# A graph network on one core: one fixed item per tile, edges counted by comparing keys, own rows on VectorE

## The chip, the core and the metric

The kernel runs on one core of a Trainium2 chip. Its engines work side by side and meet through semaphores: TensorE (PE; its weight loads are PEld), VectorE (DVE), ScalarE (ACT), GpSimd (POOL) and SyncE (SP), which here issues the plain transfers. POOL issues the gathers, transfers whose row addresses come from a table. The metric is the device time of one execution in microseconds (us), lower is better.

## The reference

50000 nodes with 256 features, 25000 directed edges, four graph layers one after another, each followed by a residual and a layer norm:

```python
x = layernorm(x + L0(x))            # sum of weight*x[dst] by src, linear, norm, relu
x = layernorm(x + L1(x, 16 kinds))  # two relational layers:
#   for each kind r: s = segment_sum(x[src]*(kind==r), dst)
#                    cnt = segment_sum(kind==r, dst)
#                    out += blockdiag(W[r]) applied to s / max(cnt, 1)
x = layernorm(x + L2(x, 24 kinds))  # two attention hops:
#   e = leaky(sum(([x[src], x[dst]] @ fc_w.T + fc_b) * rel[kind]))
#   w = softmax of e over the edges with the same src
#   x = segment_sum(x[dst]*w, src) + x;  x = x / norm(x)
x = layernorm(x + L3(x))            # interaction layer
```

## The kernel before

Nodes are cut into 391 tiles of 128 (TILES). `sort_edges` sorts the edges twice, by source and by destination, and writes records into *items*: an item holds up to 128 edges whose node is in one tile, one edge per partition. A tile has as many consecutive items as its edges need, at least one. Of these data (some 64 edges per tile) every tile has one item, so item t is tile t, but the program doesn't rely on it: `tables.make` computes for each item which tile to load (LOAD), where to store (STORE; the spare rows for all but a tile's last item), its tile's last item (LAST), whether it goes on from the item before (`keep`), and `number` computes the slot of its tile among the eight loaded (SLOT, `octet_row`). All engines read rows and slots from this table at run time, through registers.

The stages: constants and sort; `mean_layer` (l0); `count_edges_and_message` (ma); `relation_layer` (l1a); `message_phase` (mb); `relation_layer` (l1b); `attention_hop` twice (l2a, l2b); `interaction_layer` (l3). Each stage is one block in which every engine runs its own list of steps, written out in the program; there is no scheduler.

ma does two things. It makes the messages of the edges, chunk by chunk (216 chunks of 128 edges, sorted by kind, taken as 108 pairs): POOL gathers the source rows (L1098), TensorE transposes them (L1220), ScalarE copies (L1186), TensorE multiplies by the kind's block matrix (L1229), VectorE copies (L1120), SyncE stores; POOL can be 24 chunks ahead. And it finds for each edge how many edges have its destination and kind, since the mean divides by it. For 49 groups of 8 items, beside the first 48 pairs, VectorE makes one-hot matrices of node (L1111) and kind (L1106), TensorE multiplies them into counts (L1244) and ScalarE copies these (L1191). Then 16 scans over 640 items carry the counts from item to item (L1160), beside eight pairs, and in the next 48 pairs counts are looked up: the names of an item's nodes come in as rows (`ma_row`, 256 KB a group), VectorE compares them with the partition's number (`hot_t`, L1125), TensorE multiplies with the totals (L1253), and VectorE picks the kind's column (L1130, L1133). TensorE's fill in other stages is a product of zeros (`keep_busy`, L772); ma has none.

`attention_hop` works in octets of eight items. POOL gathers the eight neighbours' rows (L1989). VectorE builds the one-hot matrices and the scores (up to L2077). TensorE spreads scores and a mask over a 128x128 square per item (`spread`, L2298 and L2300), VectorE takes the maximum (L2126), and then carries a running maximum from item to item (scan L2130, `old_top`, `below` L2135, `empty`, `minus`). ScalarE takes the exponent (L2212) with its sum (`share`), and `shrink` from `minus` (L2204). TensorE turns the chances (L2307), looks up head scores (L2320) and aggregates the neighbours (L2288). The item's own row, weighted by its guarded sum, has to be added: in l2a VectorE does it (`add_self`, L2100) and then adds the item before (`add_up`, L2121: z = z_before*shrink + z). In l2b POOL makes eight diagonal matrices (L2022, L2025), TensorE multiplies them with x into the same sums (L2275), and VectorE's `add_up` (L2118) adds the item before. ScalarE squares and sums, and an inverse root follows (`inv_v` L2147, `inv_log` L1721), in l2b a second one for the layer norm (L2164). TensorE has 24 fill products an octet in l2b, 34 in l2a. The first 48 octets (24 hops) are written out one by one; what is beyond is a loop, which here runs once.

## Time and profile before

| what | us |
|---|---|
| median of 3 runs (6646.8 to 6664.31) | 6657.72 |
| span of the profiled execution, for which nothing else is given | 6924.1 |
| constants and sort | 0 to 544 |
| l0 | 552 to 1466 |
| ma | 1468 to 1896 |
| l1a | 1896 to 2594 |
| mb | 2595 to 2935 |
| l1b | 2935 to 3827 |
| l2a | 3828 to 4768 |
| l2b | 4768 to 5868 |
| l3 | 5868 to 6924 |

| engine | busy us | share |
|---|---|---|
| TensorE | 6036.3 | 87% |
| VectorE | 5018.1 | 72% |
| ScalarE | 4517.3 | 65% |
| POOL | 3702.0 | 53% |

The span is from the first to the last instruction of one profiled execution, a slower one than the timed runs. Busy time is summed over instructions. PEclk is the clock granted to TensorE as a share of full speed. An idle time before an instruction is put down to what ended it.

### The profile page before, as it was taken

Reading aid. Unit: us, or ns where it says so; the run is one execution under the profiler, and the core shown is the slowest. Engines: PE = TensorE matmul, PEld = TensorE weight load, DVE = VectorE, ACT = ScalarE, POOL = GpSimd, SP = SyncE. Lnnn points to the kernel's source line nnn. Section 1 sums busy time; section 2 is a strip of 40 time slices with the busy share of each in tenths; the row PEclk is TensorE's granted clock in tenths of the full one; section 3 lists DMA queues with packets and bytes.
Section 4 is the critical chain, followed back from the end, with each engine's and each line's share of the span. In section 5 each row is a group of like instructions: output and inputs, shape, how many; then the busy total and the mean of one; then the engine's idle time right before and its main releaser. Section 6 shows DMA issues by size and latency. Waiting matters only on the chain. (4 is left out here: it accounts for less than half of the span.)

```text
span 6924.1 us, 154954 instructions
## 1 busy us (share of the span) xinstructions
PE 6036.3 (87%) x34664; PEld 5008.9 (72%) x34665; DVE 5018.1 (72%) x17037; ACT 4517.3 (65%) x15396; POOL 3702.0 (53%) x3473
## 2 busy tenths in 40 slices
PE   6437999977899987899999788887888887999999
PEld 2226999966877775699999666665776766888888
DVE  9786999976555551277777677775666666898898
ACT  1866999952144441178888566665777776777777
POOL 0766777756366666544444444444554455444444
PEclk9658999988899998999999899998989998999999
DMA  1025777765566665577777566665666665444444
GB/s 39 2 6 162 211 210 211 211 187 163 164 184 189 192 182 166 163 215 220 218 221 219 167 203 201 198 200 158 206 198 194 196 203 175 117 127 125 126 126 119
DMA packets 1158773, 1173.00 MB, mean 169 GB/s; under 512 B 301535, under 2 KB 1032838, under 8 KB 1157701
## 3 DMA queue, kind: packets, MB, share of 16 engines
q1 hardware_dynamic: 1007108, 953.00, 45.3%
q0 software_dynamic: 151360, 216.47, 12.4%
q8 instruction: 127, 2.08, 0.1%
q14 instruction: 178, 1.45, 0.1%
HBM read 961.43 MB, written 392.14 MB: 195 GB/s over the span
## 5 line engine op out<-in xcount | busy, mean ns | idle before, releaser
L214 POOL DMA_INDIRECT landing_first<-messages,by_dst_meta x768 | 842.7, 1097 | 721.8 <-PE l1b_ps_b L1541 366.5
L214 POOL DMA_INDIRECT landing_last<-x,by_dst_meta x384 | 434.4, 1131 | 561.0 <-PE l_ps_a L1678 487.9
L1989 POOL DMA_INDIRECT landing_last<-z,by_src_meta x408 | 424.3, 1040 | 521.3 <-PE l2b_ps_g L2288 366.6
L1989 POOL DMA_INDIRECT landing_last<-x,by_src_meta x408 | 422.7, 1036 | 462.4 <-PE l2a_ps_g L2288 255.9
L214 POOL DMA_INDIRECT landing_first<-in_x,by_src_meta x384 | 407.7, 1062 | 196.7 <-PE l_ps_a L993 74.4
L1495 ACT ACTIVATE l1a_x_t<-l1a_ps_x,by_dst_first 128x256 f32<-128x256 f32 x400 | 168.0, 471 | 418.0 <-PE l1a_ps_x L1527 280.0
L1539 PE MATMUL l1b_ps_b<-root,l1b_x_t 128*128 128x256 f32 x1600 | 426.9, 389 | 1.4
L1539 PE MATMUL l1a_ps_b<-root,l1a_x_t 128*128 128x256 f32 x1584 | 418.1, 386 | 9.7 <-issue 6.1
L1003 PE MATMUL l_ps_b<-l_w,l_both 128*128 128x256 f32 x1624 | 419.3, 381 | 0.0
L1006 PE MATMUL l_ps_b<-l_w,l_agg_t 128*128 128x256 f32 x1624 | 418.0, 380 | 0.0
L1697 PE MATMUL l_ps_b<-l_w,l_mix_t 128*128 128x256 f32 x1592 | 396.6, 392 | 10.2 <-issue 7.7
L1447 DVE SCALAR_TENSOR_TENSOR l1a_total<-l1a_total,by_dst_keep,l1a_ps_b 128x256 f32<-128x256 f32 x394 | 187.1, 475 | 292.1 <-PE l1a_ps_b L1541 234.5
L1693 PE MATMUL l_ps_b<-l_w,l_x_t 128*128 128x256 f32 x1592 | 382.2, 383 | 2.5 <-ACT l_x_t L1658 2.5
L1697 PEld LDWEIGHTS l_ps_b<-l_w,l_mix_t 128*128 128x128 f32 x1592 | 286.2, 189 | 115.7 <-DVE l_mix_t L1614 63.1
L288 POOL DMA_INDIRECT item_records<-sort_rec,places x196 | 218.5, 1115 | 243.8 <-DVE places L596 184.5
L1006 PEld LDWEIGHTS l_ps_b<-l_w,l_agg_t 128*128 128x128 f32 x1624 | 309.6, 191 | 42.5
L1098 POOL DMA_INDIRECT landing_first<-x,rel_index x216 | 238.7, 1105 | 164.4 <-PE ma_ps_x L1220 83.9
L1539 PEld LDWEIGHTS l1a_ps_b<-root,l1a_x_t 128*128 128x128 f32 x1584 | 286.3, 191 | 55.0 <-issue 18.9
L772 PE MATMUL l2a_ps_g<-zero_row,ones_b 128*128 128x392 bf16 x1734 | 321.2, 329 | 1.1 <-issue 1.1
L1003 PEld LDWEIGHTS l_ps_b<-l_w,l_both 128*128 128x128 f32 x1624 | 294.1, 191 | 32.1
L1539 PEld LDWEIGHTS l1b_ps_b<-root,l1b_x_t 128*128 128x128 f32 x1600 | 289.6, 191 | 36.5 <-issue 3.7
L1693 PEld LDWEIGHTS l_ps_b<-l_w,l_x_t 128*128 128x128 f32 x1592 | 286.6, 190 | 33.8 <-ACT l_x_t L1658 2.9
(399 smaller groups left out, 19392.5 us busy)
## 6 DMA issues: line engine op xcount, KB each, us to landing
l_both<-in_x_both SPq DMA_DIRECT2D x416, 256.0 KB
l2a_x<-x SPq DMA_DIRECT2D x53, 1216.0 KB
z<-l2a_result SPq DMA_DIRECT2D x400, 152.0 KB
x<-l1b_result SPq DMA_DIRECT2D x392, 152.0 KB
l2b_x<-z SPq DMA_DIRECT2D x53, 1024.0 KB
l1b_x<-h SPq DMA_DIRECT2D x408, 128.0 KB
l1b_res<-x SPq DMA_DIRECT2D x408, 128.0 KB
l2b_res<-x SPq DMA_DIRECT2D x51, 1024.0 KB
```

Of the source, the lines that this page charges most:

```text
L214: pool.indirect_dma_start(gathered[:, slot, 0:D], None, source[0:count, :], bass.IndirectOffsetOnAxis(ap=rows, axis=0), bounds_check=limit ...
L288: self.pool.indirect_dma_start(self.target, bass.IndirectOffsetOnAxis(ap=self.place[:, column:column + 1], axis=0), self.source(column), N ...
L772: pe.matmul(spare, c.ones_b[:], c.zero_row[:], start=True, stop=True)
L1003: pe.matmul(ps_b[k % 4], x_t[:, m, i * P:(i + 1) * P], w[:, 2 + i, :], start=(i == 0), stop=False)
L1006: last = pe.matmul(ps_b[k % 4], agg_t[:, k, i * P:(i + 1) * P], w[:, i, :], start=False, stop=(i == 1))
L1098: pool.indirect_dma_start(gathered[:, slot, :], None, x_in[0:N_NODES, :], bass.IndirectOffsetOnAxis(ap=relations.index[:, chunk:chunk + 1] ...
L1447: dve.scalar_tensor_tensor(total[:, k, :], total[:, (k - 1) % RING, :], graph.keep[:, bass.ds(j, 1)], ps_b[k // 2 % 2][:, k % 2, :], ALU.m ...
L1495: act.activation(x_t[:, k, :], ps_x[k // 2 % 2][:, k % 2, :], ACT.Copy, scale=graph.first[:, bass.ds(j, 1)]).then_inc(s["xt"], 1)
L1539: pe.matmul(sums, x_t[:, k, f * P:(f + 1) * P], root[:, f, :], start=(f == 0), stop=False)
L1693: pe.matmul(ps_b[k % 4], x_t[:, k, i * P:(i + 1) * P], w1[:, i, :], start=(i == 0), stop=False)
L1697: last = pe.matmul(ps_b[k % 4], mix_t[:, k, i * P:(i + 1) * P], w2[:, i, :], start=False, stop=(i == 1))
L1989: pool.indirect_dma_start(gathered[:, k, :], None, x_in[0:N_NODES, :], bass.IndirectOffsetOnAxis(ap=rows, axis=0), bounds_check=limit, oob ...
```

## The change

Items are now laid out at fixed places: item t (t < 391) is the first item of tile t, MAIN = 392, and only tiles with more than 128 edges get all their items from number 392 on (there are none here). The item arrays grow from 640 to 896. SLOT, `octet_row` and `number` are gone. The 48 written-out octets read loads, heads and residual at constant addresses and do no scan, no `shrink`, no `add_up`; a guard is made from the maximum (`guard`). Only the loop's octets keep the carried sums, and they load each tile by its own transfer. In l2b the own rows move from POOL and TensorE to VectorE (`add_self`). In ma the 384 fixed items are counted in another way: a key is node*16 + kind; the keys of an item are loaded as a row on all partitions, and one VectorE operation per item compares the row with the partition's own key and sums the hits. The old counting with products stays for the groups from item 384 on (one here), ahead of the pairs. The look-ups shrink to one loop round of two groups. In `mean_layer` two buffers move into unused memory; its work stays.

```diff
+MAIN = TILES + 1
+MAX_ITEMS = MAIN + 2 * (N_EDGES // (P + 1))
...
+OCTETS_FIXED = HOPS_FIXED * 2
...
@@ sort_edges, buckets of each of two orders
-                    chain.step(dve.tensor_scalar(b["count"][:], b["int2"][:], 1.0, None, ALU.max))
-                    chain.step(dve.tensor_tensor_scan(b["end"][:], c.ones_row[:], b["count"][:], 0.0, ALU.mult, ALU.add))
+                    chain.step(dve.tensor_copy(b["seed"][:], b["int2"][:]))
+                    chain.step(dve.scalar_tensor_tensor(b["count"][:], b["seed"][:], 2.0, b["seed"][:], ALU.is_ge, ALU.mult))
+                    chain.step(dve.tensor_tensor_scan(b["end"][:], c.ones_row[:], b["count"][:], float(MAIN), ALU.mult, ALU.add))
                     chain.step(dve.tensor_tensor(b["base"][:], b["end"][:], b["count"][:], ALU.subtract))
-                    dve.tensor_scalar(b["seed"][:], b["base"][:], float(P), None, ALU.mult).then_inc(s_start, 1)
+                    chain.step(dve.tensor_tensor(b["seed"][:], b["base"][:], c.iota[:], ALU.subtract))
+                    chain.step(dve.scalar_tensor_tensor(b["seed"][:], b["count"][:], 2.0, b["seed"][:], ALU.is_ge, ALU.mult))
+                    chain.step(dve.tensor_tensor(b["seed"][:], b["seed"][:], c.iota[:], ALU.add))
+                    dve.tensor_scalar(b["seed"][:], b["seed"][:], float(P), None, ALU.mult).then_inc(s_start, 1)
...
@@ first message stage, VectorE
+                def compare(g, odd):
+                    if not odd:
+                        dve.wait_ge(key_in[g % 2], (g // 2 + 1) * 16)
+                    for k in range(odd * HALF, (odd + 1) * HALF):
+                        j = g * RING + k
+                        if j >= 2:
+                            dve.wait_ge(s["compared"], j - 1)
+                        dve.tensor_scalar(same[:, j % 2, :], key_row[:, g % 2, k, :], key[:, j:j + 1], 0.0, ALU.is_equal, ALU.add,
+                                          accum_out=graph.share[:, j:j + 1]).then_inc(s["compared"], 1)
...
-                for pair in range(COUNTED):
-                    last = dve.tensor_tensor_scan(total[:, r, :], graph.keep[:], total[:, r, :], 0.0, ALU.mult, ALU.add)
+                    last = dve.tensor_tensor_scan(total[:, r, :], graph.keep[:, FAST:FAST + COUNTED], total[:, r, :], 0.0, ALU.mult, ALU.add)
                     if r % 2:
-                        take_message(COUNTED + r // 2)
+                        take_message(r // 2)
                 last.then_inc(s["summed"], 1)
-                look(0, 0, 0)
-                dve.wait_ge(s["kind2"], 1)
-                for pair in range(SCANNED, LOOKED):
-                    take_message(pair)
-                    g = pair - SCANNED
-                    look_and_take(g, g % 2, g // 2)
-                for pair in range(LOOKED, PAIRS_ALL):
-                    take_message(pair)
-                with dve.Fori(COUNTED // 2, (groups + 1) // 2) as both:
+                look(FAST, 0, FAST_GROUPS // 2)
+                dve.wait_ge(s["kind2"], FAST_GROUPS + 1)
+                with dve.Fori(FAST_GROUPS // 2, (groups + 1) // 2) as both:
                     for h in range(2):
                         look_and_take(both * 2 + h, h, both)
+                for pair in range(SCANS_AT, PAIRS_ALL):
+                    take_message(pair)
+                    g, odd = divmod(pair - FIRST_LOOK, 2)
+                    if 0 <= g < FAST_GROUPS:
+                        compare(g, odd)
...
@@ first message stage, TensorE
-                    if pair < COUNTED:
-                        count(pair)
-                    elif SCANNED <= pair < LOOKED:
-                        look_up(pair - SCANNED, (pair - SCANNED) % 2)
                     if pair + 2 < PAIRS_ALL:
                         turn(pair + 2)
-                    if pair == COUNTED - 1:
-                        with pe.Fori(COUNTED, groups) as g:
-                            count(g)
-                    if pair == SCANNED - 1:
+                    if pair == SCANS_AT - 1:
                         pe.wait_ge(s["summed"], 1)
-                with pe.Fori(COUNTED // 2, (groups + 1) // 2) as both:
-                    for h in range(2):
-                        look_up(both * 2 + h, h)
+                        with pe.Fori(FAST_GROUPS // 2, (groups + 1) // 2) as both:
+                            for h in range(2):
+                                look_up(both * 2 + h, h)
...
@@ attention_hop, loads on SyncE
+                def load_tiles(octet, target, source, columns, loads):
+                    if octet.general:
+                        rows = rows_of("load", LOAD, octet)
+                        for q in range(OCT):
+                            sp.dma_start(target[:, q, :], source[bass.ds(rows[q], P), columns]).then_inc(loads[1][octet.half], 16)
+                    else:
+                        tiles = source[bass.ds(octet.item * P, OCT * P), :].rearrange("(k p) d -> p k d", p=P)
+                        sp.dma_start(target, tiles[:, :, columns]).then_inc(loads[0][octet.half], 16)
...
@@ attention_hop, POOL
-                def diagonals(octet):
...
-                    pool.tensor_tensor(diag[:, 0:own_pe, :], c.ident[:].unsqueeze(1).broadcast_to([P, own_pe, P]),
-                                       guarded[:, octet.half, 0:own_pe].unsqueeze(2).broadcast_to([P, own_pe, P]), ALU.mult)\
-                        .then_inc(s["diag"], 1)
...
@@ attention_hop, VectorE
                 def guard(o):
                     pass_wait(dve, s, s["chance"], o.item + OCT)
-                    o.wait(dve, s["empty"])
-                    dve.tensor_tensor(guarded[:, o.half, :], share[:, o.both], empty[:, o.half, :], ALU.add).then_inc(s["guarded"], 1)
+                    if o.general:
+                        o.wait(dve, s["empty"])
+                        dve.tensor_tensor(guarded[:, o.half, :], share[:, o.both], empty[:, o.half, :], ALU.add)\
+                            .then_inc(s["guarded"], 1)
+                    else:
+                        dve.scalar_tensor_tensor(guarded[:, o.half, :], peak[:, o.both], FLOOR, share[:, o.both], ALU.is_le, ALU.add)\
+                            .then_inc(s["guarded"], 1)
...
-                        dve.scalar_tensor_tensor(like_sums(q, z[:, k, :]),
-                                                 like_sums(q, x[:, bass.ds(at[q] + o.base, 1), :].rearrange("p k d -> p (k d)")),
+                        dve.scalar_tensor_tensor(like_sums(q, z[:, k, :]), like_sums(q, x[:, k, :]),
                                                 guarded[:, o.half, q:q + 1], sums(q), ALU.mult, ALU.add).then_inc(s["mixed"], 1)
...
                 def add_up(o, h):
+                    if not o.general:
+                        return
...
                 def maximum(o):
                     o.wait(dve, s["e_done"])
-                    dve.tensor_reduce(peak[:], ps_e[:], AX.X, ALU.max).then_inc(s["peak"], 1)
+                    dve.tensor_reduce(peak[:, o.both], ps_e[:], AX.X, ALU.max).then_inc(s["peak"], 1)
+                    if not o.general:
+                        o.wait(dve, s["peak"])
+                        dve.tensor_scalar(below[:, o.half, :], peak[:, o.both], -1.0, -FLOOR, ALU.mult, ALU.min)\
+                            .then_inc(s["below"], 1)
+                        return
...
-                    steps = [(add_residual, 0), (find_slots, 1), (centre, 0), (scores, 2), (part(add_up, 0), 1), (have_variance, 0), (maximum, 2)]
-                    steps += [(part(add_self, 1), 1)] if own_dve else []
-                    steps += [(part(add_up, 1), 1), (find_nodes, 3), (have_square, 1), (lambda o: inv2.square(dve, o), 0),
-                             (lambda o: inv2.weigh(dve, o), 0), (lambda o: inv2.improve(dve, o), 0), (square, 1),
-                             (weigh, 1), (shift_bias, 0), (improve, 1)]
+                    steps = [(add_residual, 0), (centre, 0), (scores, 2), (guard, 1), (part(add_self, 0), 1), (part(add_up, 0), 1),
+                             (have_variance, 0), (maximum, 2), (part(add_self, 1), 1), (part(add_up, 1), 1), (find_nodes, 3),
+                             (have_square, 1), (lambda o: inv2.square(dve, o), 0), (lambda o: inv2.weigh(dve, o), 0),
+                             (lambda o: inv2.improve(dve, o), 0), (square, 1), (weigh, 1), (shift_bias, 0), (improve, 1)]
...
@@ attention_hop, TensorE, last hop
-                    steps = [(find_slots, 3), (find_own, 1), (part(own_rows, 0), 1), (part(aggregate, 0), 1), (part(own_rows, 1), 1)]
-                    steps += [(part(own_rows, 2), 1), (part(aggregate, 1), 1), (part(aggregate, 2), 1), (part(own_rows, 3), 1)] if not own_dve else [
-                              (part(aggregate, 1), 1), (part(aggregate, 2), 1)]
-                    steps += [(spread, 2), (part(aggregate, 3), 1), (part(fill, 16), 2), (part(turn_chances, 0), 2), (look_up, 3),
-                             (part(fill, 4), 2), (part(turn_chances, 1), 2), (part(fill, 4), 2)]
+                    steps = [(part(aggregate, 0), 1), (part(aggregate, 1), 1), (part(aggregate, 2), 1), (spread, 2), (part(aggregate, 3), 1),
+                             (part(fill, 16), 2), (part(turn_chances, 0), 2), (look_up, 3), (part(fill, 4), 2),
+                             (part(turn_chances, 1), 2), (part(fill, 4), 2)]
```

VectorE in l2b before, from an octet's scores to a later octet's one-hot matrices.

```order
L2077 SCALAR_TENSOR_TENSOR l2b_score<-l2b_plain 128x8
L2118 SCALAR_TENSOR_TENSOR l2b_z<-l2b_z,l2b_shrink,l2b_ps_g 128x256 x4
L2164 TENSOR_SCALAR l2b_inv_v<-l2b_norm_squares 128x8
L2126 TENSOR_REDUCE l2b_peak<-l2b_ps_e 128x8
L2130 SCALAR_TENSOR_TENSOR l2b_top<-l2b_restart,l2b_top,l2b_peak 128x8
L2133 TENSOR_TENSOR l2b_old_top<-l2b_top,l2b_restart 128x8
L2135 TENSOR_SCALAR l2b_below<-l2b_top 128x8
L2137 TENSOR_SCALAR l2b_empty<-l2b_top 128x8
L2140 TENSOR_TENSOR l2b_minus<-l2b_old_top,l2b_top 128x8
L2143 COPY l2b_top<-l2b_top 128x1
L2118 SCALAR_TENSOR_TENSOR l2b_z<-l2b_z,l2b_shrink,l2b_ps_g 128x256 x4
L2057 TENSOR_SCALAR l2b_hot_t<-l2b_row,item_id 128x1024
```

The same stretch of VectorE after.

```order
L2084 TENSOR_REDUCE l2b_plain<-l2b_own 128x8
L2086 SCALAR_TENSOR_TENSOR l2b_score<-l2b_plain 128x8
L2096 SCALAR_TENSOR_TENSOR l2b_guarded<-l2b_peak,l2b_share 128x8
L2109 SCALAR_TENSOR_TENSOR l2b_z<-l2b_x,l2b_guarded,l2b_ps_g 128x256 x4
L2169 TENSOR_SCALAR l2b_inv_v<-l2b_norm_squares 128x8
L2127 TENSOR_REDUCE l2b_peak<-l2b_ps_e 128x8
L2130 TENSOR_SCALAR l2b_below<-l2b_peak 128x8
L2109 SCALAR_TENSOR_TENSOR l2b_z<-l2b_x,l2b_guarded,l2b_ps_g 128x256 x4
L2066 TENSOR_SCALAR l2b_hot_t<-l2b_row,item_id 128x1024
L2068 TENSOR_SCALAR l2b_mask<-l2b_row,item_id 128x1024
```

The eight additions stand at the same places, now with x and `l2b_guarded` in the place of the item before; the scan and four short operations behind the maximum are gone, so `below` follows it, and `l2b_guarded` stands ahead of the additions, which POOL made before.

TensorE in l2b before: the start of an octet's aggregation (ISA rows set an address from a register).

```order
L1831 TENSOR_LOAD by_src_table x2
L1834 ISA
L2275 ISA
L2275 MATMUL l2b_ps_g<-l2b_x,l2b_diag 128x256
L2275 ISA
L2275 MATMUL l2b_ps_g<-l2b_x,l2b_diag 128x256
L2288 MATMUL l2b_ps_g<-landing_last,l2b_hot 128x256 x2
L1834 ISA
L2275 ISA
L2275 MATMUL l2b_ps_g<-l2b_x,l2b_diag 128x256
```

TensorE in l2b after, from the aggregation to the next octet's turned chances.

```order
L2272 MATMUL l2b_ps_g<-landing_last,l2b_hot 128x256 x6
L2282 MATMUL l2b_ps_e<-l2b_mask,ident_b 128x512
L2284 MATMUL l2b_ps_e<-ident,l2b_score 128x128 x4
L2282 MATMUL l2b_ps_e<-l2b_mask,ident_b 128x512
L2284 MATMUL l2b_ps_e<-ident,l2b_score 128x128 x4
L2272 MATMUL l2b_ps_g<-landing_last,l2b_hot 128x256 x2
L788 MATMUL l2b_ps_spare<-zero_row,ones_b 128x392 x16
L2291 MATMUL l2b_ps_e<-ident,l2b_chance 128x128 x4
```

The products with `l2b_diag` and the register rows between the aggregations are gone; six aggregations stand in one piece.

VectorE in ma before, in the pairs with look-ups.

```order
L1120 COPY ma_message<-ma_ps_m 128x512
L1125 TENSOR_SCALAR ma_hot_t<-ma_row,item_id 128x1024
L1106 TENSOR_TENSOR ma_kind<-by_dst_meta,iota 128x128
L1130 TENSOR_TENSOR ma_own<-ma_kind,ma_ps_e 128x128
L1133 TENSOR_REDUCE by_dst_share<-ma_own 128x8
L1120 COPY ma_message<-ma_ps_m 128x512
```

VectorE in ma after: the end of the loop round with look-ups, and the pairs with compares behind it, which go on in this way.

```order
L1176 TENSOR_REDUCE by_dst_share<-ma_own 128x8
L1181 REGISTER_ALU
L1210 ISA
L1210 COMPARE_AND_BRANCH
L1152 COPY ma_message<-ma_ps_m 128x512 x2
L1162 TENSOR_SCALAR ma_same,by_dst_share<-ma_key_row,ma_key 128x128 x4
L1152 COPY ma_message<-ma_ps_m 128x512
```

Between two message copies stood the wide comparison with the partition's number and the pick of a column, which waits for TensorE; now four compares stand there, which wait for no other engine.

## Rows read from the trace of the kernel before

**Rows 1.** Windows, one for each stage; the columns stand in the first row:

```profile
core 0: us, PE busy (x) PEld busy (x) DVE busy (x) ACT busy (x) POOL busy (x), PEclk, DMA share, GB/s
...
1466.00:1896.00 430.00, 324.19 (x2498) 300.57 (x2498) 255.88 (x531) 83.11 (x216) 238.68 (x216) 0.81 0.57 168
...
2934.00:3827.00 893.00, 879.46 (x5564) 800.78 (x5564) 647.10 (x2588) 719.76 (x1987) 428.42 (x408) 0.99 0.73 217
...
4768.00:5868.00 1100.00, 956.76 (x5186) 757.40 (x5186) 734.91 (x2420) 815.43 (x3207) 552.55 (x532) 0.90 0.64 194
```

**Rows 2.** What POOL waited for, 147 to 545 us: total, times, longest:

```profile
POOL item_records L288 <- DVE places L596: 184.5, 5, 152.8
```

**Rows 3.** Groups of VectorE's instructions by line and shape, 358 to 405 us:

```profile
L376 DVE TENSOR_SCALAR_CACHE_REDUCE sort_in_relation<-dst_end,item_id 128x391 f32<-128x391 f32 x5 | 3.1, 620 | 3.5 <-remote 2.2 <-DVE by_src_groups L396 1.3
...
L391 DVE TENSOR_TENSOR sort_tmp<-sort_tmp 128x5 f32<-128x5 f32 x2 | 0.3, 167 | 0.6 <-DVE sort_tmp L390 0.5
```

**Rows 4.** Windows inside the first message stage:

```profile
1500.00:1652.00 152.00, 99.62 (x917) 86.31 (x916) 101.33 (x234) 43.84 (x141) 112.30 (x100) 0.82 0.55 163
1685.00:1850.00 165.00, 154.57 (x1082) 151.32 (x1082) 80.49 (x191) 22.86 (x39) 79.53 (x76) 0.80 0.62 172
```

**Rows 5.** Line L1098, the gathers of the first message stage: ns, first and last start:

```profile
L1098 POOL DMA_INDIRECT landing_first<-x,rel_index x216: 1006/1012/1680, 1468.7 to 1847.5; - x108
```

**Rows 6.** Line L1329, the gathers of the second message stage:

```profile
L1329 POOL DMA_INDIRECT landing_first<-h,rel_index x216: 1004/1012/1027, 2595.0 to 2913.2; - x108
```

**Rows 7.** Groups by line and shape, 1466 to 1896 us, first message stage:

```profile
L1106 DVE TENSOR_TENSOR ma_kind<-by_dst_meta,iota 128x128 f32<-128x128 f32 x51 | 14.5, 284 | 0.0
```

**Rows 8.** Timeline of TensorE in the first message stage: start, length:

```profile
1673.74 1.15 PE L1229 MATMUL ma_ps_m<-ma_wide,ma_x_t 128*128 x8 [1.77 <-DVE ma_message L1120]
1674.73 0.60 PE L1220 MATMUL ma_ps_x<-ident,landing_first 128*128 128x128 f32 x4
1680.85 2.07 PE L1229 MATMUL ma_ps_m<-ma_wide,ma_x_t 128*128 x8 [5.51 <-DVE ma_message L1120]
...
1691.98 1.09 PE L1220 MATMUL ma_ps_x<-ident,landing_first 128*128 128x128 f32 x4
```

**Rows 9.** Windows inside the two attention stages:

```profile
3900.00:4600.00 700.00, 617.58 (x3927) 467.69 (x3927) 533.14 (x1381) 470.06 (x1804) 330.16 (x320) 0.99 0.66 200
4860.00:5760.00 900.00, 797.62 (x4311) 631.07 (x4309) 624.89 (x2065) 692.35 (x2717) 450.79 (x431) 0.91 0.66 199
```

**Rows 10.** Timeline of one octet of the first attention stage:

```profile
4329.97 0.67 PE L2288 MATMUL l2a_ps_s<-landing_last,l2a_hot 128*128 128x304 f32 x2
...
4331.47 1.01 POOL L1989 DMA_INDIRECT landing_last<-x,by_src_meta  x1 [4.83 <-PE l2a_ps_s L2288]
...
4339.26 4.87 SPq L1939 DMA_DIRECT2D z<-l2a_result  x8
...
4341.15 0.36 DVE L2070 TENSOR_TENSOR l2a_both<-l2a_ps_s,landing_last 128x192 f32<-128x192 f32 x1 [0.36 <-DMA landing_last<-x,by_src_meta]
...
4346.31 0.68 PE L2288 MATMUL l2a_ps_s<-landing_last,l2a_hot 128*128 128x304 f32 x2
```

**Rows 11.** Waits in the first attention stage, 3900 to 4600 us:

```profile
ACT l2a_chance L2212 <- DVE l2a_below L2135: 62.8, 40, 2.7
...
DVE l2a_both L2070 <- DMA landing_last<-x,by_src_meta: 23.8, 31, 2.4
```

**Rows 12.** Groups by line and shape, 4860 to 5760 us, second attention stage:

```profile
L2275 PE MATMUL l2b_ps_g<-l2b_x,l2b_diag 128*128 x692 | 186.1, 404 | 19.2 <-POOL l2b_diag L2025 17.4 <-issue 1.6
...
L2212 ACT ACTIVATE l2b_chance<-l2b_ps_e,l2b_below 128x128 f32<-128x128 f32 x344 | 121.0, 377 | 83.0 <-DVE l2b_below L2135 41.6 <-issue 41.4
...
L2025 POOL TENSOR_TENSOR l2b_diag<-ident,l2b_guarded 128x1024 f32<-128x1024 f32 x44 | 83.9, 1906 | 3.4
...
L2147 DVE TENSOR_SCALAR l2b_inv_v<-l2b_total_sq 128x8 f32<-128x8 f32 x44 | 45.6, 1038 | 83.6 <-DMA x<-l1b_result 38.2 <-ACT l2b_squares L2199 34.1 <-issue 11.3
...
L1721 ACT ACTIVATE l2b_inv_log<-l2b_inv_v 128x8 f32<-128x8 f32 x87 | 17.6, 202 | 72.1 <-DVE l2b_inv_v L2147 68.5 <-issue 3.0
```

420 lines of the change are left out of this document (191 added, 229 removed).

## Prediction

> **What bounds the kernel now.** I read the page's busy shares first: TensorE is busy 87% of the span, VectorE 72%, ScalarE 65%, POOL 53%, so no engine is full all the time and the bound has to be found stage by stage. I then cut the span into stages with the windows view (the stage table above, its rows for three stages in [rows 1]), and inside each stage read the groups by line and shape, the waits and one octet or pair on the timeline. The change touches the sort, the first message stage (430 us), the first attention stage (941 us) and the second (1100 us). The other stages issue the same work as before and I leave them at their time.
>
> In the sort POOL waits 184.5 us for VectorE's places, 152.8 of it in one piece [rows 2]: VectorE is on the path before the scatters.
>
> In the first message stage the time changes hands twice. While counts are made (1500 to 1652 us) 100 gathers take 152 us, 1.52 each. While the counts are looked up (1685 to 1850) TensorE is busy 154.6 of 165 us and only 76 gathers are issued, 2.17 each [rows 4]. The look-up is what fills TensorE there, at a mean granted clock of 0.80. The second message stage does the same messages with no counting: its 216 gathers start from 2595.0 to 2913.2, 1.48 each [rows 6], against 1468.7 to 1847.5, 1.76 each, in the first [rows 5].
>
> In the first attention stage 320 gathers are 40 octets in 700 us, 17.5 us each, with TensorE busy 15.4, VectorE 13.3, ScalarE 11.8 [rows 9]. No engine is full; what closes is a loop. An octet's aggregation ends at 4330.64 (4329.97 + 0.67), that frees slots and a gather starts at 4331.47, VectorE sees the landing at 4341.15, then come scores, spread and the next aggregation, which ends at 4346.99 [rows 10]: 16.35 us.
>
> In the second attention stage 344 chances are 43 octets in 900 us, 20.9 us each, with TensorE busy 18.5, ScalarE 16.1, VectorE 14.5 [rows 9, 12]. ScalarE is idle 83.0 us before the chances, half of it put on VectorE's `below`, and 72.1 before `inv_log`, which waits for VectorE's `inv_v` [rows 12]. That op is 8 elements wide and yet takes 1038 ns, while POOL runs the diagonals, 1906 ns each, once per octet. VectorE's short op stands behind POOL's long one.
>
> **The change part by part.** The sums go against the profiled execution, whose span is 6924.1 us; the page gives no time outside the span. The median of the runs is 6657.72, 3.8% less, so I scale the sum by 6657.72/6924.1 = 0.962.
>
> Sort: four more bucket operations per direction, eight in all. The nearest row is a 391-wide operation of 0.620 us [rows 3]: +5.0. The tables need 36 wide reductions instead of 30, +3.7, and about 28 more operations of the 0.167 kind, +4.7 [rows 3]. With the gaps of a dependent chain I take +15, from +8 (the scatters cover part, since those in flight while the tables are made don't wait) to +30 (every small operation pays a wait). The item records grow from 640 to 896 rows and are loaded before the first layer: 0.7 MB at the 168 GB/s of [rows 1] is 4 us, part of it covered by the weights' loads; I take +2.5, between 0 and +5.
>
> First message stage: the 16 look-up products per pair on TensorE go, and so do nearly all counts and their copies. What is left on TensorE per pair is four transposes and eight products, 0.60 + 1.15 = 1.75 us at full clock and 1.09 + 2.07 = 3.16 at the half one [rows 8]. VectorE gets 384 compares of 128 columns with an accumulator. The trace has none of this form. A 128x128 operation without accumulator takes 0.284 [rows 7], a 391-wide one with it 0.620 [rows 3]. I take 0.35, four per pair, 1.4 us, plus a message copy near 0.7: 2.1 per pair on VectorE, below POOL's pair. The bound above, 0.620, gives 3.2 per pair, which would be VectorE-bound: 96 pairs x 3.2 = 307 us. So POOL sets the pace as in the second message stage: first start 1468.7, 215 x 1.48 = 318, and a tail of 22 (the second message stage ends at 2935, its last gather starts at 2913.2) end at 1809, against 1896: -87. The second message stage has no key loads, though: each two pairs load 256 KB broadcast over the partitions, the bytes of the row loads before. With them the count stretch ran 1.52 and moved 163 GB/s, so they may cost something. I add 15 for that and for the compares beside POOL. Result -72, bounds -87 and -30. The upper bound is VectorE or TensorE at 3.2 per pair for the 96 pairs with compares, 307, with some 40 us of first pairs and scans, and the tail of 48 that the stage had (1847.5 to 1896): 395 us of 430, in round numbers.
>
> The trace doesn't show how compares and gathers share memory. In the count stretch, where VectorE is busy 101.3 of 152 us, POOL's gathers are 1.12 each instead of 1.01 [rows 4, 6]. The Trainium skill, page "SBUF — State Buffer", section "Who interferes with whom", says that the `tensor_scalar` form that writes out its accumulator does not take the port pair shared with GpSimd, unlike the plain form. By the rule the compares would not lengthen a gather, and the 15 us above would shrink towards 0; by the row of the count stretch they would cost 0.11 x 216 = 24. No run here shows it yet.
>
> First attention stage: VectorE loses eight operations over 304 columns and five small ones per octet. VectorE is not the bound. ScalarE's waits for `below` are 62.8 us over 40 octets, 1.6 each [rows 11], and those mostly go, but the gather loop of 16.35 stays whole: none of its links is removed. It also carries landings that come late (23.8 us over 31 waits, 0.6 per octet [rows 11]). I take 16.8 us instead of 17.4: 49 octets x 0.6 = -29; bounds -34 (everything at 16.7) and 0 (the landing sets it as now).
>
> Second attention stage, the largest term. Per octet:
> TensorE loses the own-row products, 186.1/43 = 4.3 us [rows 12], and the register work ahead of them: 18.5 becomes 14.2. POOL loses the diagonals (1.9). VectorE issues as many 256-wide additions as before, with x in the place of the carried sum, and loses scan, `old_top`, `empty` and `minus`. ScalarE loses one 8-wide activation (0.2, as L1721's shape): 16.1 becomes 15.9, and is now the fullest engine. Of ScalarE's 4.8 us idle (900 - 692.35 over 43), `inv_log` has 72.1/43 = 1.7, of which I let 1.5 go because `inv_v` no longer stands behind the diagonals (0.83 for the operation alone, the rest its queue), and chances have 83.0/43 = 1.9, of which 1.3 goes since `below` follows the reduction directly. 15.9 + 4.8 - 2.8 = 17.9, and I take 18.1 for the longer way of `guard`, which now stands on VectorE between scores and additions. (20.9 - 18.1) x 49 = -137; bounds T = 16.5 (-216, ScalarE full but for 0.6) and T = 20.0 (-44, if transfers hold it).
>
> Cover lost: own rows were products that kept TensorE awake, see the rival below. The last, general octets load x, heads and residual with eight DMAs instead of one; SyncE needs 4.87/8 = 0.61 per issue [rows 10], 21 more per octet in the last hop, on a queue that runs ahead by octets: +6, between 0 and +15. Stores wait behind them.
>
> Sum: 15 + 2.5 - 72 - 29 - 137 + 6 = -214.5; scaled -206: 6658 - 206 = 6452 us.
>
> **The rivals.**
> B, transfers take over. The second attention stage moves 199 GB/s now [rows 9]; at 18.1 us an octet it would need 230. The most in any stage is 217 GB/s, in the second relation stage [rows 1]. At 217 the octet is 20.9 x 199/217 = 19.2, and since its loads stand in bursts I take 19.5: -69. With the message stage at -40 and the first attention stage at -10 the sum is -95, scaled -91: 6567 us. For it: late landings are already seen [rows 11]. Against: DMA share is 0.66, not 0.73 as in that stage.
> C, all at the floors: -216, -87, -34, and +20 for sort and loads: -317, scaled -305: 6353 us. Against: the remaining waits of a chain through five engines rarely vanish together.
> D, slower: the clock of TensorE falls in the second attention stage. It is granted 0.91 there now, with 89% busy [rows 9], and without the own rows TensorE works 14.2 us of 18.1. At 1.2 GHz throughout the 14.2 us become 14.2 x 0.91 x 2 = 25.8 us, more than any other engine has, and the octet lasts 25.8: +240 there, with the rest -77, so +163, scaled +157: 6815 us. It decides once the mean granted clock is under 14.2 x 0.91/20.9 = 0.62. For it: after 5.51 us without work the clock halved in the message stage (eight products 1.15 before, 2.07 after [rows 8]). Against: 24 fill products remain in each octet, and the gaps get shorter, not longer. The Trainium skill, page "TensorE: Matmul & The Clock Gate", section "HAM oscillation — how this bites in real kernels", states that an engine whose bursts are shorter than the waits between them is gated down again each time. By this rule the loss of the own rows speaks for D; the trace of the half-speed products agrees with the mechanism, not with its taking hold in an octet that is 78% busy.
> E, the fixed path gains nothing because the path it shortens isn't the one that ends last (the sort's +15 and message stage's compares at 0.620 eat the rest): -20 to +20, 6658.
>
> **How the numbers follow.** Forecast 0.60, B 0.21, C 0.10, D 0.04, E 0.05. The forecast's own range is 6400 to 6520; B reaches to 6600, C to 6350, so 6350 to 6600 holds about 0.85. A change of 0.3% (20 us) is about what can be told from none. Faster: 0.60 + 0.21 + 0.10 + a little of E = 0.92; same 0.03; slower 0.05.
>
> **What would show it.** The first message stage should last about 358 us with gathers at 1.48 to 1.55 us and POOL no longer waiting for the transposes for long; a compare between 0.28 and 0.62 us. The second attention stage should come at about 960 us, ScalarE the fullest, `inv_v` near 0.2 us, and no POOL work beside the gathers. The first attention stage should be 910 us with VectorE near 8.5 us of each octet. If the second attention stage stays above 1050 us, with ScalarE and TensorE idle before a landing, B was right; if TensorE's clock there is under 0.7, D. If the sort grows by more than 30 us, my chain costs are wrong.

## The result and the profile after

The changed kernel runs in 6409.3 us (median of 4 runs, 6406.93 to 6410.99); the kernel before ran in 6653.1 us beside it. The ratio is 0.963, 95% interval 0.9617 to 0.9644: 3.7% faster, 244 us. The forecast was 6452 us, 206 us less. The time lies in the range.

```profile
span 6409.2 us, 146244 instructions
...
PE 5644.9 (88%) x32700; PEld 4709.4 (73%) x32701; DVE 4652.7 (73%) x16722; ACT 4457.7 (70%) x15208; POOL 3534.5 (55%) x3365
...
PEclk9668999998899999999999899998999998999999
```

The page of the kernel after: span, busy time, and the rows by slices. TensorE is as full as before (88% of the span, 87% then). In the five slices that lie whole in the second attention stage the core moves 234 to 252 GB/s, where it moved some 200 before.

One thing has to be known before stages are compared. The kernel before was timed on several chips: on one of them seven runs took 6904 to 6935 us ("the slower chip" below), on two others 6632 to 6650 ("the faster chips"). The profile that the prediction rests on has a span of 6924.1 us and stages as long as those of the slower chip; this result is from a chip on which the kernel before took 6653.1. A second profile of the kernel before, on a faster chip, has a span of 6637.0 us. The table has the time from each stage's first gather or load to the next one's. The changed kernel itself was not run on the slower chip: there the column after is put together from kernels of the experiments in which that stage is the changed kernel's, unaltered. By that column the change gains as much on the slower chip (some 3.5%), but not in the same stages. The stages of the two faster profiles differ by 227.8 us in all, the medians of the runs by 244; the 16 us between them stand in no stage.

| stage | before, 6637.0 us | after, 6409.2 us | difference | slower chip: before, 6924.1 us | slower chip: after | difference |
|---|---|---|---|---|---|---|
| sort | 518.8 | 519.6 | +0.8 | 556.1 | 563.0 to 574.5 | +7 to +18 |
| l0 | 903.3 | 903.3 | 0.0 | 912.6 | 915 | +2 |
| ma | 397.6 | 300.4 | -97.2 | 428.7 | 348.5 to 350.4 | -79 |
| l1a | 675.7 | 681.8 | +6.1 | 697.6 | 698 | 0 |
| mb | 292.4 | 290.6 | -1.8 | 341.1 | 342 | +1 |
| l1b | 883.6 | 883.9 | +0.3 | 893.6 | 891 to 896 | -3 to +3 |
| l2a | 918.3 | 873.3 | -45.0 | 942.4 | 937 | -5 |
| l2b | 1002.9 | 907.0 | -95.9 | 1100.5 | 932.3 to 934.3 | -167 |
| l3 | 1044.4 | 1049.3 | +4.9 | 1051.5 | 1047 | -4 |

The stages l1a and l3 issue the same work in both; between the changed kernel and its variants on the faster chips they lie at 669.5 to 681.8 and 1044.8 to 1049.3 us, so 5 us there mean nothing.

The windows of the kernel after that answer to [rows 1, 4, 9], columns as there: the first message stage, the second one, and stretches inside the first and second attention stage.

```profile
1422.00:1722.00 300.00, 202.32 (x1350) 179.28 (x1350) 209.56 (x916) 67.45 (x124) 220.35 (x216) 0.85 0.81 242
2404.00:2697.00 293.00, 258.44 (x1872) 204.60 (x1872) 75.59 (x111) 63.37 (x108) 216.93 (x217) 0.97 0.64 192
3650.00:4350.00 700.00, 656.78 (x4260) 505.32 (x4259) 368.03 (x954) 493.67 (x1913) 349.89 (x350) 1.00 0.71 216
4530.00:5250.00 720.00, 606.61 (x3623) 487.06 (x3624) 526.57 (x1900) 683.94 (x2678) 361.22 (x347) 0.92 0.82 248
```

The same four places in the second profile of the kernel before:

```profile
1422.00:1819.00 397.00, 314.88 (x2498) 296.15 (x2498) 253.56 (x532) 83.99 (x216) 240.55 (x216) 0.84 0.61 182
2495.00:2787.00 292.00, 259.37 (x1872) 205.15 (x1872) 74.68 (x108) 63.20 (x108) 217.85 (x216) 0.97 0.64 192
3800.00:4500.00 700.00, 610.82 (x3978) 475.15 (x4017) 544.07 (x1416) 484.70 (x1846) 335.47 (x328) 1.00 0.67 205
4690.00:5410.00 720.00, 661.98 (x3774) 524.97 (x3811) 548.86 (x1811) 612.39 (x2397) 402.53 (x383) 0.96 0.72 220
```

The second attention stage: 344 chances in 720 us are 43 octets, 16.7 us each, against 38 (304 additions) in 720, 18.9 us each. VectorE is busy 12.2 us an octet after and 14.4 before. ScalarE is busy 95% of the stretch. TensorE's clock fell from 0.96 to 0.92. The first attention stage: 350 gathers, 43.7 octets, 16.0 us each, against 41 (328 gathers), 17.1 us each.

TensorE's only waits in these two stretches of the first attention stage, before and then after, are for the scores (total, times, longest):

```profile
PE l2a_ps_e L2300 <- DVE l2a_score L2077: 89.1, 41, 3.3
```

```profile
PE l2a_ps_e L2282 <- DVE l2a_score L2086: 43.2, 43, 2.2
```

That is 2.2 us an octet before and 1.0 after, while TensorE's work stays near 15 us an octet, fill products included: the octet of the first attention stage got shorter by what TensorE waits less for VectorE's scores.

Groups of the kernel after, first message stage, which answer to [rows 5, 7]: the gathers, and the compares, which are the new operation.

```profile
L1130 POOL DMA_INDIRECT landing_first<-x,rel_index x216 | 220.4, 1020 | 86.7 <-issue 55.4 <-POOLq L124 21.2 <-PE ma_ps_x L1255 10.1
...
L1162 DVE TENSOR_SCALAR_CACHE_REDUCE ma_same<-ma_key_row,ma_key 128x128 bf16<-128x128 f16 x384 | 109.4, 341 | 13.4 <-DMA ma_key_row<-node_rows 13.3
...
L1162 DVE DVE_READ_ACCUMULATOR ma_same<-ma_key_row,ma_key 128x1 f32 x384 | 31.8, 83 | 0.0
```

A compare takes 341 ns (0.35 was forecast) and 83 more to read the accumulator. Gathers wait 10.1 us for TensorE in all (55.1 in the second profile of before); 216 of them start in 284.9 us, 1.33 us each.

Groups of the second attention stage after, which answer to [rows 12]:

```profile
L2160 DVE SCALAR_TENSOR_TENSOR l2b_result<-l2b_z,l2b_inv_root,l2b_res 128x256 f32<-128x256 f32 x344 | 143.8, 482 | 15.4 <-DVE l2b_inv_root L1775 10.5 <-DMA l2b_res<-x 4.9
L2109 DVE SCALAR_TENSOR_TENSOR l2b_z<-l2b_x,l2b_guarded,l2b_ps_g 128x256 f32<-128x256 f32 x347 | 143.4, 475 | 11.8 <-DVE l2b_guarded L2096 11.8
...
L2221 ACT ACTIVATE l2b_chance<-l2b_ps_e,l2b_below 128x128 f32<-128x128 f32 x344 | 120.7, 375 | 15.2 <-DVE l2b_below L2130 15.0
...
L2282 PE MATMUL l2b_ps_e<-l2b_mask,ident_b 128*128 128x512 bf16 x88 | 42.4, 482 | 102.8 <-DVE l2b_score L2086 102.8
...
L1758 ACT ACTIVATE l2b_inv_log<-l2b_inv_v 128x8 f32<-128x8 f32 x86 | 17.4, 203 | 10.6 <-DVE l2b_inv_v L2153 10.6
...
L2282 PEld LDWEIGHTS l2b_ps_e<-l2b_mask,ident_b 128*128 128x128 bf16 x88 | 9.9, 112 | 120.4 <-DVE l2b_score L2086 120.4
...
L2153 DVE TENSOR_SCALAR l2b_inv_v<-l2b_total_sq 128x8 f32<-128x8 f32 x43 | 7.8, 182 | 77.5 <-ACT l2b_squares L2206 77.5
```

`inv_v` takes 182 ns, ScalarE waits 10.6 us for it and 15.0 for `below`. In [rows 12], over 900 us, these two were 68.5 and 41.6, but in the second profile of the kernel before, 4690 to 5410 us, they were only 4.0 and 52.6. What is new is TensorE's wait for the scores, 102.8 us.

### The profile page after: what moved, and what is told of

Read it like the earlier page. It is cut to its first block and busy times, and to the rows that moved or that the text cites. A ratio compares the mean times of both kernels' runs of the same rounds, so it can differ in the third digit from the quotient of the medians.

```text
span 6409.2 us, 146244 instructions
## 1 busy us (share of the span) xinstructions
PE 5644.9 (88%) x32700; PEld 4709.4 (73%) x32701; DVE 4652.7 (73%) x16722; ACT 4457.7 (70%) x15208; POOL 3534.5 (55%) x3365
## 5 line engine op out<-in xcount | busy, mean ns | idle before, releaser
L215 POOL DMA_INDIRECT landing_first<-messages,by_dst_meta x768 | 826.4, 1076 | 665.2 <-PE l1b_ps_b L1578 368.2
L843 ACT ACTIVATE l_norm_junk<-l_summed,l_norm_minus_mean 128x256 f32<-128x256 f32 x392 | 196.0, 500 | 139.2 <-DVE l_norm_minus_mean L834 139.2
```

What stands on the lines that cost most here:

```text
L215: pool.indirect_dma_start(gathered[:, slot, 0:D], None, source[0:count, :], bass.IndirectOffsetOnAxis(ap=rows, axis=0), bounds_check=limit ...
L843: act.activation(self.junk[:, k % self.junk_slots, :], values[:, k, :], ACT.Square, bias=self.minus_mean[:, k:k + 1], accum_out=self.squar ...
```

## Experiments

All but before_again are edits of the changed kernel, timed beside the kernel before; the ratio is to that. before_again, lookups_back, carry_back and own_rows_back ran on one of the faster chips, own_rows_2, pool_diag_2, pe_own_2 and apply4 on the other, and no_compare, pool_diag_only, pe_own_only and idle_adds on the slower chip. Differences of a stage are against the changed kernel's stage on a faster chip (873.3 and 907.0 us for the attention stages) or against the column of the slower chip. The six runs of own_rows, pool_diag and pe_own also keep ScalarE's array of squares in bf16 instead of f32, to make room; an operation on it takes 423 to 425 ns either way.

**before_again** is the kernel before without an edit.

> The kernel before, unchanged, for a second profile. Theory: the profiled execution of 6924 us was 4% slower than the runs because it was a slowed one, also where the two kernels issue the same work. Then a new profile lies near 6650 us, and the second message stage, whose code is the same in both kernels, gathers at about 1.31 us (281 us for 216) as in the kernel after, not at 1.48. Rival: the second message stage is really slower in the kernel before, by something that the ma stage leaves behind; then it stays at 1.48. What remains between this profile and the one after is the change: I expect the first message stage at 400 us against 300, the first attention stage at 900 against 870, the second at 1050 against 908.

One run of 6638.78 us, span 6637.0. The second message stage takes 292.4 us (gathers at 1.31 us) as in the kernel after, so its 341 is nothing that the code of the kernel before does. The theory held in its numbers. Its "slowed execution" turned out to be the slower chip, where kernels with this stage unchanged take 341.7 to 342.5 us for it. The first message stage came at 398, the first attention stage, forecast at 900, at 918, and the second, forecast at 1050, at 1003.

**lookups_back** puts eight look-up products of the old shape in 48 pairs of the first message stage.

```diff
+ if FIRST_LOOK <= pair < FIRST_LOOK + FAST_GROUPS:
+     for k in range(RING):
+         pe.matmul(ps_dummy[:, k * R1:(k + 1) * R1], hot_t[:, 1, k, :],
+                   total[:, :, k:k + 1]..., start=True, stop=True)
```

> The changed kernel with eight idle look-up products (sixteen passes of 128x16) put back on TensorE in 48 pairs of the first message stage, in the places where the look-ups stood; their results are used by nobody. Own theory (the look-ups made TensorE the bound): pairs of 3.6 to 4.3 us in place of 2.6, +50 to +85 us in that stage, clock in it lower or equal. Rival (the loads and VectorE's waits held the stage before, not TensorE): under +15 us.

6419.24 us, ratio 0.9665 (0.9649 to 0.9681); first message stage 325.3 us, +25. The window:

```profile
1500.00:1690.00 190.00, 180.14 (x1583) 174.41 (x1581) 122.82 (x638) 43.01 (x74) 129.69 (x130) 1.00 0.81 233
```

TensorE is full (180 of 190 us) at a clock of 1.00, and a pair takes 3.07 us on its timeline. So TensorE did become the bound, as the theory said, but for 25 us and not for 50 to 85, and with a higher clock and not a lower one (0.88 in the same stretch of the kernel after). TensorE of before_again, start and length in us, two pairs with look-ups and the products of a third:

```profile
1700.88 3.59 PE L1253 MATMUL ma_ps_e<-ma_total,ma_hot_t 128*128 x16
1704.31 1.09 PE L1220 MATMUL ma_ps_x<-ident,landing_first 128*128 128x128 f32 x4
1705.19 1.89 PE L1229 MATMUL ma_ps_m<-ma_wide,ma_x_t 128*128 x8
1706.90 1.88 PE L1253 MATMUL ma_ps_e<-ma_total,ma_hot_t 128*128 x16
1708.62 0.63 PE L1220 MATMUL ma_ps_x<-ident,landing_first 128*128 128x128 f32 x4
1709.09 1.06 PE L1229 MATMUL ma_ps_m<-ma_wide,ma_x_t 128*128 x8
```

The look-ups at 3.59, the transposes at 1.09 and the products at 1.89, 6.57 us together, are at 1.2 GHz; then the same at 1.88, 0.63 and 1.06, 3.57 together, at 2.4 GHz. The mean pair takes 4.2 us there (66 gathers in 140 us), at a granted clock of 0.81. VectorE waits for the names in that stretch, 1640 to 1780 us (total, times, longest):

```profile
DVE ma_hot_t L1125 <- DMA ma_row<-node_rows: 38.6, 25, 2.4
```

TensorE's products wait 7.0 us there for the comparison that follows the names, and its weight loads 10.7 us for nothing that the profile shows.

Products alone cost 25 of the 97 us. The other 72 are not taken apart by an experiment, so their cause is not shown. The profiles show two candidates. One is the half clock and the waits for name rows (together 1.1 us a pair over 3.07). The other is that in the count stretch gathers last longer, beside VectorE's `tensor_tensor` operations that make the one-hot matrices. The groups of POOL are at 1450 to 1600 us of before_again and, beside the compares, at 1500 to 1690 us of the kernel after:

```profile
L1098 POOL DMA_INDIRECT landing_first<-x,rel_index x101 | 119.7, 1185 | 30.8 <-issue 26.5 <-PE ma_ps_x L1220 4.3
```

```profile
L1130 POOL DMA_INDIRECT landing_first<-x,rel_index x146 | 146.1, 1000 | 44.5 <-issue 36.5 <-PE ma_ps_x L1255 7.9
```

**no_compare** leaves out the compares and their key loads (the counts stay at one, so messages are not divided).

```diff
- if 0 <= g < FAST_GROUPS:
-     compare(g, odd)
```

> The changed kernel without the 384 compares and without the key loads of the first message stage (12 MB less in transfers); the counts stay at one, so messages aren't divided by them. Theory (POOL's gathers set the pace at 1.3 us each, compares run beside them): first message stage within 6 us of 300. Rival (compares take the memory ports from POOL, or the key loads delay the landings of the gathers): 15 to 25 us shorter.

On the slower chip 6684.81 us against 6925.23 for before, ratio 0.9664 (0.9634 to 0.9695). Its first message stage lasts 344.6 us, against 348.5 to 350.4 in the three other kernels of this chip. Compares and key loads cost 4 to 6 us together; they run beside the gathers. The forecast 300 was for a faster chip; that the stage would move by no more than 6 us held. What the compares cost on a faster chip, where POOL is quicker, was not tried.

**carry_back** brings back the carried sums in the written-out octets of both hops.

```diff
 def add_up(o, h):
-    if not o.general:
-        return
 def maximum(o):
-    if not o.general: ... return        # below from the peak alone
 def measure(o, first, n):
-    act.wait_ge(s["mixed"], j + 1)
+    act.wait_ge(s["added"], j + 2)
```

> The changed kernel with the carried sums back in the 48 written-out octets of both hops: scan, old_top, empty, minus, shrink and add_up on VectorE, all else as after. Own theory (the first hop is held by its gather loop, the second by ScalarE): first hop +0.6 to +1.0 us per octet, +30 to +50 us; second hop: VectorE rises from 12.2 to about 17.4 us an octet, above ScalarE's 15.9, so the octet goes from 16.7 to about 19, +110 us. Sum +150 us, near 6560. Rival (transfers hold both hops, VectorE's work is free): under +30 us. Rival (everything VectorE loses was on the path): +5.2 us an octet in both, +500 us.

6683.22 us, ratio 1.0065 (1.0048 to 1.0082): slower than the kernel before. First attention stage 921.4, +48, which is all of the 45 us that it had gained. TensorE's wait for the scores is back there as well, 3650 to 4350 us:

```profile
PE l2a_ps_e L2268 <- DVE l2a_score L2086: 88.3, 41, 3.1
```

So in this stage the carried sums on VectorE stood between TensorE and its scores. Second attention stage 1140.1, +233, more than twice what was expected. There VectorE now adds twice for each item, the own row and then the item before, 16 additions an octet; the kernel before had one addition for both, since TensorE made the own rows. So this stage is not the one of the kernel before. Windows in the second and the first of them:

```profile
4600.00:5500.00 900.00, 717.43 (x3457) 566.86 (x3498) 682.39 (x2341) 669.65 (x2640) 341.38 (x336) 0.77 0.64 192
3650.00:4350.00 700.00, 611.67 (x3978) 478.36 (x4017) 540.47 (x1415) 480.61 (x1846) 336.51 (x329) 0.99 0.68 205
```

42 octets in 900 us are 21.4 us each, and no engine is full: VectorE 76%, ScalarE 74%. The granted clock of TensorE is 0.77, the lowest of all stretches here, though above the 0.7 that the prediction had named as the sign of its rival D. How much of the 233 us the clock costs, and how much the longer chain over VectorE, is not shown.

**own_rows_back** and **own_rows_2** are one kernel, run twice: the own rows of the second hop by POOL's diagonals and TensorE's products, with no carried sums; VectorE's additions stay, with a factor of zero. POOL also makes `guarded`, as before, and VectorE one 8-wide operation (`empty`) for it.

```diff
+ pool.tensor_tensor(diag[:], ident..., guarded[:, octet.half, :]..., ALU.mult)
+ pe.matmul(out, diag[:, q, :], x[:, k, cols], start=(q % 2 == 0), stop=False)
- dve...(z, x, guarded[:, o.half, q:q + 1], sums(q), ALU.mult, ALU.add)
+ dve...(z, x, nothing[:], sums(q), ALU.mult, ALU.add)
```

> The changed kernel with the own rows of the second hop made by POOL's diagonals and TensorE's products again, no carried sums. VectorE still issues its eight additions (with a factor of zero). Own theory (POOL's diagonals hold up VectorE's short operations and TensorE has 4.3 us more per octet): second hop from 16.7 to 19.5 us an octet, +137 us, inv_v back to about 1 us, near 6550. Rival (the carried sums and not the own rows were what cost): under +30 us. The other stages unchanged.

> The own rows of the second hop back on POOL and TensorE, as in own_rows_back, beside the two single parts on one chip. If each part cost by itself what it did alone (79 and 90 us), and they add up, the second hop is 165 us longer than after; if both lie in one chain and TensorE is the bound with either, 80 to 95.

6489.08 us, 0.9774 (0.9758 to 0.9791), and 6487.75, 0.9769 (0.9753 to 0.9785). The second attention stage is 990.4 and 990.3 us, +83: 87% of the stage's gain is the own rows' move. 13 us are left for all else in this stage, the scan and short operations of the carried sums and the constant addresses; the carried sums needed no additions of their own there. Expected were 137, and `inv_v` at about 1 us, which stayed at 172 ns.

**pool_diag_only** and **pool_diag_2**: POOL makes an idle array of the diagonals' shape once per octet; nobody waits.

```diff
+ pool.wait_ge(s["chance"], octet.item + OCT)
+ pool.tensor_tensor(diag[:], ident..., graph.keep[:, 0:OCT]..., ALU.mult)
```

> The changed kernel, and in the second hop POOL makes an idle array of the diagonals' shape (128x1024, ident times a column) once per octet at the place of the diagonals; nobody waits for it. Theory of the prediction (VectorE's short operations stand behind it, inv_v at 1 us): second hop +40 to +80 us. Rival, from the second profile of the kernel before, where inv_v took 196 ns beside the diagonals: under +12 us, and inv_v near 0.2 us.

> POOL's idle diagonals alone, again. Theory (what POOL's 1.9 us cost depends on whether they fall on VectorE's short operations and on the gathers' issue; the machine on which the first profile of before was taken is the one on which the short operations fell behind them): second hop +10 to +80 us, with inv_v's mean above 0.3 us where it is long and near 0.2 where it is short. Rival (the cost is POOL's own time in the gather loop, independent of VectorE): +70 to +80 us again, inv_v near 0.2 us.

On the slower chip 6764.63 us, 0.9779 (0.9757 to 0.9801), second attention stage 1012.4, +79, with `inv_v` at 1342 ns: the theory held there. On the faster 6506.57, 0.9794 (0.9777 to 0.981), 1007.1, +100, 2.0 us an octet for 1.9 us on POOL. Where these go, in VectorE's groups of pool_diag_2, 4530 to 5250 us:

```profile
L2168 DVE TENSOR_SCALAR l2b_inv_v<-l2b_total_sq 128x8 f32<-128x8 f32 x39 | 54.4, 1396 | 66.2 <-ACT l2b_squares L2221 66.2
...
L1770 DVE SCALAR_TENSOR_TENSOR l2b_inv_b<-l2b_inv_a,l2b_inv_v 128x8 f32<-128x8 f32 x78 | 43.2, 553 | 2.9
```

`inv_v` takes 1396 ns instead of 182, and `inv_b` 553 instead of 167. VectorE's busy time goes from 12.2 to 14.3 us an octet, though it does the same work. In own_rows_2 `inv_v` is short and the residual's additions are long (482 in the kernel after):

```profile
L2187 DVE SCALAR_TENSOR_TENSOR l2b_result<-l2b_z,l2b_inv_root,l2b_res 128x256 f32<-128x256 f32 x316 | 187.5, 654 | 10.8 <-DVE l2b_inv_root L1775 10.8
```

and so in before_again, where 305 of them at 137 ns more are 1.1 us an octet:

```profile
L2155 DVE SCALAR_TENSOR_TENSOR l2b_result<-l2b_z,l2b_inv_root,l2b_res 128x256 f32<-128x256 f32 x305 | 170.8, 619 | 17.2 <-DVE l2b_inv_root L1738 17.2
...
L2025 POOL TENSOR_TENSOR l2b_diag<-ident,l2b_guarded 128x1024 f32<-128x1024 f32 x39 | 74.4, 1907 | 3.1
...
L2147 DVE TENSOR_SCALAR l2b_inv_v<-l2b_total_sq 128x8 f32<-128x8 f32 x38 | 7.5, 196 | 44.4 <-ACT l2b_squares L2199 44.4
```

So in each of these profiles VectorE instructions are longer beside POOL's diagonal, by 1 to 2 us an octet together; which instruction pays differs, also between two profiles of the kernel before (`inv_v` 1038 ns in one, 196 in the other). The second expectation forecast 10 to 80 us by the chip, its rival 70 to 80 with a short `inv_v`; 100 us with a long one is neither.

**pe_own_only** and **pe_own_2**: TensorE multiplies with eight zero matrices at the places of the own-row products; POOL does nothing.

```diff
+ pe.matmul(out, diag[:, q, :], x[:, k, cols], start=(q % 2 == 0), stop=False)   # diag is zero
```

> The changed kernel, and in the second hop TensorE multiplies x with eight constant zero matrices into the sums, sixteen passes an octet, where the own-row products stood; POOL makes nothing, VectorE still adds the own rows. Theory (TensorE's 4.2 us are on the path: 14.1 + 4.2 = 18.3 us an octet against ScalarE's 15.9): second hop +75 to +90 us, nearly all of what bringing back both cost (83). Rival (TensorE has slack, only POOL's diagonals in its chain cost): under +25 us.

> TensorE's sixteen idle own-row passes alone, again. Theory (TensorE becomes the bound at 18.3 us an octet): second hop +75 to +90 us also here. Rival (it depends on the machine as POOL's part does): under +50 us.

On the slower chip 6779.89 us, 0.9798 (0.9778 to 0.9817), second attention stage 1023.5, +90: as expected. On the faster 6384.27 us, 0.9612 (0.9595 to 0.9628), stage 887.7: 19 us *less* than after. That missed the theory, and the rival had it. Its window:

```profile
4530.00:5250.00 720.00, 713.82 (x4414) 598.41 (x4457) 540.81 (x1959) 701.82 (x2774) 366.66 (x359) 1.00 0.84 255
```

The clock is 1.00 instead of 0.92, an octet takes 16.0 us, ScalarE is busy 97% and TensorE 99%. The idle products take 3.9 us an octet (174.5 us for 45), and all other products together went from 14.1 to 12.0. The spread products, which VectorE's maximum and the chances wait for, show it, first the kernel after and then pe_own_2:

```profile
L2284 PE MATMUL l2b_ps_e<-ident,l2b_score 128*128 128x128 f32 x697 | 126.0, 341 | 0.0
```

```profile
L2296 PE MATMUL l2b_ps_e<-ident,l2b_score 128*128 128x128 f32 x720 | 94.9, 275 | 5.7 <-DVE l2b_score L2087 3.4
```

They take 341 ns in the mean behind the wait for the scores, and 275 where the idle products fill that wait (TensorE's 102.8 us for the scores are 3.4 here). Work that yields nothing makes the stage shorter. 6384 is the lowest median of all kernels here, but it was not timed side by side with the changed kernel (6409), and the intervals of the two ratios overlap (0.9617 to 0.9628). Why the same edit costs 90 us on the slower chip stays open; at 4750 to 5470 us there TensorE is busy 93% at a clock of 0.95, and VectorE's `inv_v` waits 35.3 us for a landing of x, which it does not on the faster chip.

The three edits together on that faster chip: the idle diagonals cost 100 us, the idle products gain 19, and both with their real use (own_rows_2) cost 83, close to the 81 of the sum. So there the gain from moving the own rows is about what POOL's diagonals had cost. The 80 to 95 us that the expectation of own_rows_2 gives for TensorE as the bound held in the number, by luck, and not in the reason. On the slower chip, where each part alone costs 79 and 90, the two together were not run.

**idle_adds**: in the first hop VectorE does eight additions of `add_up`'s shape into an array that nobody reads.

```diff
+ dve.scalar_tensor_tensor(idle[:], z[:, (k - 1) % HOP, :], guarded[:, o.half, 0:1], z[:, k, :], ALU.mult, ALU.add)
```

> The changed kernel, and in the first hop VectorE does eight additions of the shape of add_up in its place, each after the one before, into an array that nobody reads; scan, below and shrink stay out. Bringing back all of the carried sums cost 48 us there. Theory (the additions stand ahead of the next scores on VectorE and so in the gather loop): +30 to +45 us. Rival (the longer way to below and ScalarE's wait for the added sums cost): under +12 us.

On the slower chip 6682.47 us, 0.9655 (0.9635 to 0.9675); first attention stage 940.4 against 936.7 to 937.6 of the other three, +3. But the whole change gives that stage only 5 us there. Its theory missed and its rival held. But the run can't say what part of the carried sums made up the 45 on the faster chip: there TensorE waited for the scores (89.1 us before), while in the first profile of before its 64.5 us at the same place are put down to nothing that the profile shows and only 12.7 to the scores.

**apply4** moves the last normalisation of four items an octet from ScalarE to VectorE, to beat both kernels.

```diff
+ dve.tensor_scalar(result[:, k, :], result[:, k, :], inv2.root[:, k:k + 1], norm.bias[:, k:k + 1],
+                   ALU.mult, ALU.add).then_inc(s["out_dve"], 1)        # at the end of VectorE's steps
```

> The changed kernel, and in the second hop VectorE does the last normalisation (scale and bias, L2241) of four of the eight items, ScalarE the other four. Theory (ScalarE, busy 95% of the second hop after, is its bound): ScalarE loses 2.0 us of 16.7 per octet, VectorE gains 1 to 2 of its 12.2; octet at 15.0 to 15.5 us, second hop 60 to 80 us shorter, ratio to the kernel before 0.951 to 0.954. Rival (transfers at 248 GB/s or the gather loop hold it as much as ScalarE): under 20 us.

6446.62 us, 0.9708 (0.9691 to 0.9724), faster than the kernel before and slower than the changed one; second attention stage 956.8, +50. Window and wait:

```profile
4530.00:5250.00 720.00, 579.19 (x3356) 483.16 (x3396) 547.88 (x1952) 569.20 (x2346) 334.09 (x324) 0.88 0.78 235
```

```profile
PE l2b_ps_e L2295 <- DVE l2b_score L2090: 140.8, 41, 4.2
```

ScalarE got its relief (569 of 720 us) and the octet still grew to 17.8 us: TensorE waits 3.4 us an octet for the scores (2.3 after), which now stand behind four more operations on VectorE. Neither the theory nor the rival foresaw it. That ScalarE was 95% busy did not make it the engine to relieve; the chain over VectorE's scores was as near, and ScalarE itself now waits 92.4 us for VectorE's `norm_minus_mean` (1.1 after). The clock fell too, from 0.92 to 0.88.

## Why the prediction came out right, point by point

**Sort, forecast +15 and +2.5.** On the faster chip +0.8, on the slower +7 to +18. The bucket part is there. POOL's wait for VectorE's places, before_again and then the kernel after:

```profile
POOL item_records L288 <- DVE places L596: 152.8, 1, 152.8
```

```profile
POOL item_records L289 <- DVE places L609: 157.6, 1, 157.6
```

4.8 us more, where 5.0 were forecast. The tables' part was mis-sized for the faster chips. In [rows 2] POOL waited five times, here once: the scatters before it cover the tables, and they end at 500.8 us before and 499.8 after.

**First message stage, forecast -72, measured -97 (-79 on the slower chip).** That POOL sets the pace held: 1.33 us a gather after, 1.31 in the second message stage of this chip. The mis-sized terms are the 1.48 [rows 6], which is the slower chip's pace, and the 15 us added for key loads and compares, which cost 4 to 6 (no_compare). Gathers of 1000 ns in the mean beside the compares agree with the rule that was weighed from the Trainium skill, page "SBUF — State Buffer", section "Who interferes with whom": the form with an accumulator leaves the shared ports alone. That the look-up products were what filled the stage before was right in part: alone they cost 25 us.

**First attention stage, forecast -29, measured -45 (-5).** The mechanism was wrong in two steps. The gather loop of 16.35 us was named as what stays whole, "none of its links is removed", and VectorE as not the bound; but the scores are a link of that loop, and TensorE's wait for them went from 2.2 to 1.0 us an octet, came back with carry_back, and the octet went to 16.0 us. And ScalarE's waits for `below`, which were mostly to go, stayed. Before_again and the kernel after, in the stretches above:

```profile
ACT l2a_chance L2212 <- DVE l2a_below L2135: 54.1, 41, 1.6
```

```profile
ACT l2a_chance L2221 <- DVE l2a_below L2130: 69.3, 44, 3.2
```

That the stage came near the forecast is luck. On the slower chip it hardly moved; what holds it there is not shown.

**Second attention stage, forecast -137, measured -96 (-167).** The step with `inv_v` behind POOL's diagonals was right in its mechanism: the idle diagonals alone cost 79 and 100 us. It was wrong to take the length of one instruction, 1038 ns, as the place, and the 1.5 us of `inv_log`'s wait with it; in before_again `inv_v` takes 196 ns, `inv_log` waits 4.0 us for it in all and the residual's additions pay. The step with 1.3 us for `below` was nearly right in size (its wait went from 52.6 us over 38 octets to 15.0 over 43, 1.0 us an octet), but not in its cause: in own_rows_2, which has no carried sums either, ScalarE still waits 39.2 us for `below` over 39 octets, so most of it went with the own rows. TensorE's 4.3 us, which the sum did not count as path, are no cost on the faster chip. Not in the sum at all is TensorE's new wait for the scores, 2.3 us an octet, with its lower clock: pe_own_2, where both are gone, is 19 us shorter.

**Rivals.** B: 248 to 255 GB/s were moved, above the 217 that the rival took as the most, so it fell. D: in the changed kernel the clock went to 0.92 and the octets shortened nonetheless, so it did not take hold; it came nearest in carry_back, with 0.77. The Trainium skill, page "TensorE: Matmul & The Clock Gate", section "HAM oscillation — how this bites in real kernels", describes how waits between short bursts of matmuls bring the clock down each time. The windows agree with it in direction only: in pe_own_2, after and carry_back TensorE is idle 0.1, 2.6 and 4.3 us an octet, at clocks of 1.00, 0.92 and 0.77, but in all three it works far longer than it waits, and pool_diag_2 has 4.5 us of idleness at 0.91. C, all floors: the result lies 43 us below the forecast and 56 above C, so it is nearly as close to the one as to the other. E, nothing gained, fell.

**The scale.** The sum was made against 6924.1 us and multiplied by 0.962, as if the slower chip were slower everywhere. It is slower in the stages with gathers and scatters and little else (sort 7%, first message stage 8%, second 17%), 10% in the second hop, 3% in l1a and the first hop, and hardly in l0, l1b and l3 (1%). By luck the errors partly cancel: too little for the message stage and first hop, too much for the second and the sort.

## What to carry to other kernels

When an engine's short instruction is long in one profile, look for what another engine runs beside it, and cost the other engine's whole instruction, not the victim: the victim differs between profiles. Before taking work from TensorE, see what it will wait for then and what its clock does; on one of two chips idle products were worth more than none. When a loop passes over an engine that is not full, ask what stands ahead of the loop's link in that engine's list. Before a sum is scaled from one profile to other runs, compare a stage that does not change.

## What was not expected of the hardware

- The same program takes 6640 us on one chip and 6925 on another. A third of the loss is in the second attention stage, and most of the rest in the sort, the message stages and the first hop: 216 gathers start in 318.2 us on the slower and in 282.4 on the other, while their own length is 1.01 us on both.
- An idle POOL operation of 1.9 us costs 2.0 us an octet, though POOL is busy for half of the time and nobody waits for it.
- Sixteen idle passes on TensorE an octet gain 19 us on one chip (clock 0.92 to 1.00) and cost 90 on the other.
